# A gated recurrence: where its splits, loads and fills stand, and a fifth pair of each layer turned by DMA

## The reference

```python
for i in range(n_layers):          # 6
    gate = ih[i][token]            # (2048, 256), token clamped to the table
    state = jnp.tanh(state + jnp.matmul(state, hh[i]) * gate)
return state
```

## Time and profile before

| what | us |
|---|---|
| median of 3 runs | 105.71 |
| lowest and highest | 105.27, 107.05 |
| the profiled execution | 106.02 |
| its span, first to last instruction | 104.2 |
| PE busy in the span | 87.1 (84%) |
| DVE busy | 79.2 (76%) |
| ACT busy | 73.5 (70%) |
| POOL busy | 65.7 (63%) |

### The profile page before, as it was taken

The page is one execution under the profiler, slowest core; times in us unless marked ns, Lnnn a source line. Parts: engine busy times, 40 slices in busy tenths (PEclk is TensorE's granted clock), DMA queues, the critical chain, the costliest instruction groups (busy, mean ns, idle before and its releaser), DMA issues.

```text
span 104.2 us, 1794 instructions
## 1 busy us (share of the span) xinstructions
PE 87.1 (84%) x650; PEld 74.4 (71%) x650; DVE 79.2 (76%) x127; ACT 73.5 (70%) x129; POOL 65.7 (63%) x60
## 2 busy tenths in 40 slices
PE   5919909895498998987999989999899998999900
PEld 5817608474386896976898978999789897898800
DVE  2179085283979399996979879798897978989990
ACT  4078020891897818799799996999969999667431
POOL 2687787734043008694897939979398893992440
PEclk9995885589999999999999999999999999999998
DMA  3899999999699915542387523555319654095355
GB/s 39 285 367 401 417 388 376 315 307 347 205 215 268 188 36 101 104 79 48 75 58 145 97 60 58 101 101 101 72 29 86 121 101 94 18 130 221 147 201 201
DMA packets 27128, 17.46 MB, mean 168 GB/s; under 512 B 22421, under 2 KB 22677, under 8 KB 27120
## 3 DMA queue, kind: packets, MB, share of 16 engines
q1 hardware_dynamic: 24816, 13.64, 55.2%
q0 software_dynamic: 2304, 3.71, 9.9%
HBM read 19.14 MB, written 2.10 MB: 204 GB/s over the span
## 4 chain that ended last, share of the span: by engine, by line
PE 51%; DMA 16%; DVE 13%; issue 9%; SPq 3%; ACT 3%; POOL 2%; POOLq 0%; DVEq 0%
PE products L278 38%; PE turned L310 7%; DMA state<-in_state_rows 6%; DVE sums L434 5%; DMA gates<-in_gate_rows,index 5%; PE products L270 5%; DMA w_full<-in_weights 5%; DVE sums L442 4%; ACT gates L336 1%; POOL sums L262 1%; DVE split_rows L455 1%; DVE split_cols L448 1%; ACT state L372 1%; SPq L190 1%; POOL gates L255 1%
## 5 line engine op out<-in xcount | busy, mean ns | idle before, releaser
L262 POOL TENSOR_TENSOR sums<-sums,state 128x512 f32<-128x512 f32 x37 | 46.8, 1274 | 21.4 <-DVE sums L434 20.5
L278 PE MATMUL products<-w_head,split_cols 128*128 128x256 f16 x316 | 54.8, 273 | 1.5 <-issue 1.5
L372 ACT ACTIVATE state<-sums 128x512 f32<-128x512 f32 (+1 forms) x49 | 30.2, 619 | 19.9 <-DVE sums L442 10.9
L278 PE MATMUL products<-w_rest,split_cols 128*128 128x256 f16 x158 | 43.1, 273 | 0.0
L278 PEld LDWEIGHTS products<-w_head,split_cols 128*128 128x128 f16 x316 | 30.9, 98 | 5.8 <-issue 2.3
L434 DVE SCALAR_TENSOR_TENSOR sums<-products,w_down,gates 128x512 f32<-128x512 f32 (+1 forms) x40 | 29.3, 735 | 0.3 <-PE products L278 0.2
L270 PE MATMUL products<-w_full,first_cols 128*128 128x256 f32 x64 | 20.1, 471 | 8.7 <-DMA first_cols<-in_state_cols 6.0
L270 PEld LDWEIGHTS products<-w_full,first_cols 128*128 128x128 f32 x64 | 14.5, 237 | 13.6 <-DMA first_cols<-in_state_cols 7.4
L255 POOL DMA_INDIRECT gates<-in_gate_rows,index x13 | 14.3, 1099 | 10.2 <-ACT gates L336 6.8
L278 PEld LDWEIGHTS products<-w_rest,split_cols 128*128 128x128 f16 x158 | 15.4, 98 | 1.7
L455 DVE SCALAR_TENSOR_TENSOR split_rows<-copies,split_rows 128x512 f16<-128x512 f32 x19 | 13.0, 686 | 3.9 <-ACT split_rows L360 3.7
(11 more groups left out here) (30 smaller groups left out, 28.5 us busy)
## 6 DMA issues: line engine op xcount, KB each, us to landing
first_cols<-in_state_cols SPq DMA_DIRECT2D x8, 256.0 KB, 5.0
state<-in_state_rows SPq DMA_DIRECT2D x8, 256.0 KB, 5.9
out<-state SPq DMA_DIRECT2D x7, 256.0 KB, 2.0
w_full<-in_weights SPq DMA_DIRECT2D x6, 256.0 KB, 5.2
last_row<-in_gate_rows SPq DMA_DIRECT2D x1, 768.0 KB, 4.6
split_cols<-split_rows SPq DMA_TRANSPOSE x19, 3.1
gates<-in_gate_rows,index POOLq DMA_INDIRECT x16, 5.5
out<-state SPq DMA_DIRECT2D x2, 128.0 KB, 1.9
```

The costliest lines, as they stand in the source:

```text
L262: nc.gpsimd.tensor_tensor(sums[:, q], sums[:, q], pair_rows(state, q), ALU.add).then_inc(pool_added, 1)
L278: last = nc.tensor.matmul(bank[:, j, :], split_cols[:, q, s, j, k, :], w[:, l - 1, k * HID:(k + 1) * HID], start=(n == 0), stop=(n == len( ...
L372: nc.scalar.activation(pair_rows(state, q)[:, cut], sums[:, q, cut], ACT.Tanh).then_inc(state_ready, 1)
```

## The change

- Pair 4 of the layers 0 to 4 is turned by DMA too, so there are five turns by DMA in a layer and three by PE. Unlike the other four, pair 4 gets no second tanh into PSUM: its head and its rest are made from `state` in SBUF. `copied`, `state_copies`, `rests_with_copy` and `split_from` count and choose accordingly.
- SP loads the columns one step further ahead (`load_cols(2)` before the steps), one layer of weights with each step's loads instead of two, and the last two pairs of rows together at step 5.
- Six fills on DVE and four on ACT stand before the steps (five and three before), then ACT fills tile 13 after step 0 and tile 15 after step 1, DVE tile 14 after step 0.
- The head of the next layer's weights is made three steps earlier (9, 17, 25, 33), its rest likewise (10, 18, 26, 34). The second sum product stands at step 8.
- Pair 6 of the last layer is added on DVE, not POOL.

```diff
--- before.py
+++ after.py
@@ -33,7 +33,9 @@
     END = STEPS - 1


-    DMA_PAIRS = (1, 3, 5, 7)
+    DMA_PAIRS = (1, 3, 4, 5, 7)
+
+    COPY_PAIRS = (1, 3, 5, 7)
     LAST_TURN = (LAST - 1, PAIRS - 1)

     TURN_LAG = 3
@@ -41,20 +43,20 @@
     REST_LAG, REST_ROWS_LAG = 4, 2


-    LAST_ON_DVE = (3, 5, 7)
+    LAST_ON_DVE = (3, 5, 6, 7)

     WHOLE = 3
-    ACT_FILLS = {-1: (4, 7, 10), 1: (12,), 3: (14,)}
-    DVE_FILLS = {-1: (3, 5, 6, 8, 9), 0: (11,), 2: (13,), 3: (15,)}
+    ACT_FILLS = {-1: (4, 6, 9, 11), 0: (13,), 1: (15,)}
+    DVE_FILLS = {-1: (3, 5, 7, 8, 10, 12), 0: (14,)}


     GROUPS = ((0, 1), (1, SPLIT))
     SUMS_AT = {0: 0, 2: 1, 3: 2, 4: 3, 5: 4}
-    TOTALS_AT = {3: 0, 9: 1}
-    HEADS_AT = {3: 0, 12: 1, 20: 2, 28: 3, 36: 4}
-    RESTS_AT = {4: 0, 13: 1, 21: 2, 29: 3, 37: 4}
+    TOTALS_AT = {3: 0, 8: 1}
+    HEADS_AT = {3: 0, 9: 1, 17: 2, 25: 3, 33: 4}
+    RESTS_AT = {4: 0, 10: 1, 18: 2, 26: 3, 34: 4}

     WARM = 9
     TOP = 14
@@ -70,6 +72,16 @@

     def by_pe(i):
         return order[i][0] < LAST and not by_dma(i)
+
+    def copied(i):
+        return by_dma(i) and order[i][1] in COPY_PAIRS
+
+    def state_copies(i):
+        return sum(copied(n) for n in range(i + 1))
+
+
+    def rests_with_copy(n):
+        return dma_turns([i for i in range(STEPS) if copied(i)][n - 1])

     def on_pool(i):
         layer, q = order[i]
@@ -179,7 +191,10 @@
             return turned[(pe_turns(i) - 1) % TURNED]

         def copy_bank(i):
-            return copies[(dma_turns(i) - 1) % COPIES]
+            return copies[(state_copies(i) - 1) % COPIES]
+
+        def split_from(i):
+            return copy_bank(i)[:, :, :] if copied(i) else pair_rows(state, order[i][1])

         block = ctx.enter_context(nc.Block())

@@ -202,18 +217,16 @@
             load_weights(0)
             load_cols(1)
             load_rows(0)
+            load_cols(2)
             for i in range(STEPS):
-                if i + 2 < PAIRS:
+                if i + 3 < PAIRS:
                     sp.wait_ge(product_ready, i + 1)
-                    load_cols(i + 2)
+                    load_cols(i + 3)
                     load_rows(i + 1)
-                    if i == 0:
-                        load_weights(1)
-                    elif i <= 2:
-                        load_weights(2 * i)
-                        load_weights(2 * i + 1)
-                elif i + 2 == PAIRS:
+                    load_weights(i + 1)
+                elif i + 3 == PAIRS:
                     load_rows(i + 1)
+                    load_rows(i + 2)
                 if i >= LOAD_LAG and by_dma(i - LOAD_LAG):
                     q = order[i - LOAD_LAG][1]
                     sp.wait_ge(rest_rows_ready, dma_turns(i - LOAD_LAG))
@@ -356,8 +369,11 @@

             def make_head_rows(i):
                 q = order[i][1]
-                act.wait_ge(copy_ready, dma_turns(i))
-                nc.scalar.activation(split_rows[:, q, 0], copy_bank(i)[:, :, :], ACT.Copy,
+                if copied(i):
+                    act.wait_ge(copy_ready, state_copies(i))
+                else:
+                    act.wait_ge(state_ready, i + 1)
+                nc.scalar.activation(split_rows[:, q, 0], split_from(i), ACT.Copy,
                                      scale=STATE_SCALE).then_inc(head_rows_ready, 1)

             def new_state(i):
@@ -370,9 +386,9 @@
                     if n >= 1:
                         act.wait_ge(vector_added, vector_adds(i) + n)
                     nc.scalar.activation(pair_rows(state, q)[:, cut], sums[:, q, cut], ACT.Tanh).then_inc(state_ready, 1)
-                if by_dma(i):
-                    if dma_turns(i) > COPIES:
-                        act.wait_ge(rest_rows_ready, dma_turns(i) - COPIES)
+                if copied(i):
+                    if state_copies(i) > COPIES:
+                        act.wait_ge(rest_rows_ready, rests_with_copy(state_copies(i) - COPIES))
                     nc.scalar.activation(copy_bank(i)[:, :, :], sums[:, q], ACT.Tanh).then_inc(copy_ready, 1)

             for t in ACT_FILLS[-1]:
@@ -452,7 +468,7 @@
             def make_rest_rows(i):
                 q = order[i][1]
                 dve.wait_ge(head_rows_ready, dma_turns(i))
-                nc.vector.scalar_tensor_tensor(out=split_rows[:, q, 1], in0=copy_bank(i)[:, :, :], scalar=STATE_SCALE,
+                nc.vector.scalar_tensor_tensor(out=split_rows[:, q, 1], in0=split_from(i), scalar=STATE_SCALE,
                                                in1=split_rows[:, q, 0], op0=ALU.mult,
                                                op1=ALU.subtract).then_inc(rest_rows_ready, 1)

```

## The result

| | before | after |
|---|---|---|
| median of 4 runs, us | 105.53 | 112.38 |
| lowest and highest | 105.27, 107.05 | 111.02, 112.98 |
| profiled execution and its span | 106.02, 104.2 | 112.30, 110.5 |

The ratio is 1.061, with a 95% interval of 1.049 to 1.074. Single executions of one kernel can take some per cent longer than the rest at a lower granted clock; all ratios here leave these out, while the medians are over all executions. The forecast was 98.6 us, and 112.38 lies 10 us above the end of the range.

A forecast was written before the change was run, and what follows sets the result against it. Loads were taken to bound the kernel to about 37 us, PE from 44.91 to 93.84, DVE the end. Savings 4.2 + 2.8 + 0.1 = 7.1 us off the profiled 106.02 gave 98.9, as a median 98.6; range 96.0 to 102.3.

The forecast's parts named there:

- the chain is PE's own: From 44.91 to 93.84 us PE's own work was taken to set the layer, busy 12.45 of 12.74 us.
- The four turns, -1.8: In PE's chain, dropping pair 4's turn by PE from four layers saves 4 x 0.44 = 1.8 us.
- DVE and the lock: Two DVE instructions per layer may wait for POOL's add; half an add, twice, is absorbed by 1.57 us of DVE idle.
- rival (4): Slower: both new DVE instructions wait a whole POOL add, 2.54 us a layer, giving 110.9 us; chance 0.03.
- a swap at 0.06 us: In each layer, DVE's rest of pair 4 from SBUF instead of PSUM costs 0.06 us more.
- The stalls, -2.1: Weights three steps earlier remove PE's stalls before layers (1.5 us) and restarts (0.6); half of 2.1 us was counted.
- The front, -4.2: Until step 7: earlier gathers and loads, all landed between 31.3 and 34.1 us, bring step 7's gated 4.2 us earlier.
- are issued earlier too: In the front, the last rows, issued by 31.28 before, no longer wait for a product of their own.
- The point at which the prediction called itself wrong: The prediction is wrong if the last gather still lands after 34 us, or a layer stays over 12.4.
- PE is no obstacle: In the front, with columns one step ahead, PE's product of step 7 ends well before its gates need it.
- I take this piece as rigid: From step 7's gates to PE's turn at 44.91 us: earlier gates make that turn earlier too.
- The end, -0.1: Last adds: one whole DVE add more (0.69 us) against a lost wait for POOL (0.78 us), -0.1 us.

The follow-up runs named there:

- e9: Kernel before, with only one of pair 4's four PE transposes in layers 1 to 4; executions between 104.95 and 107.74 us, no ratio.
- e10: Kernel before, with the later layers' weights' head at steps 10, 18, 26, 34 and rest at 12, 20, 28, 36; 106.17 us, ratio 1.004.
- e12: Kernel before plus pair 4 turned by DMA from state, its rest first in a step, weights' head and rest at steps 10 and 12 and so on; 106.64 us, 1.004.
- e6: Kernel before plus pair 4 turned by DMA from state, its rest put ahead of the PE-turned pair's rest in a step; 108.35 us, ratio 1.014.
- e7: Kernel before plus one unused DVE copy from PSUM ahead of pair 7's gated in layers 1 to 4; 108.38 us, ratio 1.014.
- e5: Kernel before plus pair 4 turned by DMA from state, at late places: head three steps behind, rest four, transpose five; 113.29 us, no interval.
- e3: Changed kernel with four pairs turned by DMA, without the fifth, keeping the new fills, loads and weights' steps; 107.50 us, ratio 1.013.
- e13: Changed kernel with four pairs by DMA, last row loads ahead of the first transpose, which waits until last rows and gates have landed; 107.71 us, 1.017.
- e11: Changed kernel with four pairs by DMA and the last row loads ahead of SP's first DMA transpose, which is not held; 108.76 us, 1.023.
- e14: Changed kernel with four pairs by DMA, rows first, first transpose held until inputs land, and the old weights' steps; 108.24 us, no interval.

## Why the prediction was wrong

**The step that failed** is the first section's "From there to 93.84 us the chain is PE's own" with "A layer takes 12.74 us, in which PE is busy for 12.45". PE was nearly full and had a stall of only 0.28, and I read that as a bound with a small hitch. It was the other way: what ended the hitch was the bound. What closes each layer is a loop of 12.74 us that PE meets once: the rest of the weights and the `gated` on DVE, the adds on POOL, tanh and head on ACT, the rest on DVE, and so on to the next layer's weights. The kernel before was balanced to 2%, and the busy share could not tell which of two nearly equal bounds was the longer. e9 tells it: 0.33 us less PE work, 0.33 more stall.

**The four turns, -1.8.** Measured: nothing. In e9 PE's work fell and the layer did not; e10 and e12 take 12.85 and 12.88 with four and with five pairs. The instructions went as said.

**DVE and the lock.** That half a POOL add, twice, "is just absorbed" by 1.57 us of idle time of DVE is the second failure, and the more costly. That idle time was waiting for ACT inside the loop, at other places than the new instruction; 0.60 us of work between the `gated` of pairs 6 and 7 was paid whole (e6, e7). Measured is 0.60 for the rest of pair 4 as work and 0.70 for its wait for POOL, 1.30 a layer. The wait itself lay inside my bounds of 0 and 1.27. So rival (4), slower, with a chance of 0.03, was the one that came: 110.9 against 112.38. Its condition, that DVE must lose more than its idle time and a whole add for each of two instructions, was wrong; one instruction and half an add were enough. That its number came near is luck: it had 9.5 of loss and 4.3 of gain, where by the first table the layers lost 7.4 and the front and the end gave 1.1. I also took the second rest for a swap at 0.06 us. It has the old one's length, but stands two steps earlier in the program, and place counted ten times as much as length.

The Trainium skill, page SBUF — State Buffer, section Who interferes with whom, says that a DVE instruction with two SBUF inputs and a GpSimd instruction that reads SBUF contend, and the later is blocked. The traces agree, also for this kind of instruction: 1.38 and 1.72 where DVE came second, 0.68 where it came first and POOL took 1.65 (e5: 0.69, and 1.77 on POOL). I had weighed the rule and given it half; what was wrong was to set it against idle time.

**The stalls, -2.1, half taken.** PE's stall before a layer did go, but a layer became 0.27 longer (e3), not shorter. At the earlier steps the loop holds three ACT instructions more (a head, a tanh and a second tanh, 1.50 us in all, as from 70.97 to 72.46 in the changed kernel) and one POOL add of 1.27 less, and DVE waits 0.71 for the head of the weights (0.44 before). With e10's steps it is 12.85, still no gain. Which arrangement would open the loop stays open.

**The front, -4.2.** Measured: -0.2 in one trace of each kernel, and step 7 varies by 3 us between executions; but over the six kernels with the new loads and no held transpose it is never before 36.4. The first half of the reasoning held: the last gather started at 24.78, forecast 24.8, and where nothing disturbed them, the loads were in at 33.85 (e13), inside my 31.3 to 34.1. Two terms were missing. One is SP's queue: the last loads of rows stood behind a transpose whose issue took 5.07 us, so that "are issued earlier too" came down to 29.02 against 30.37. The other is the time to landing: I used 5.40 for a gather, and beside transposes it was 10.4 in the changed kernel and 12.2 in e11. By e3 and e11 these two stand behind one another, each hiding the other. The point at which the prediction called itself wrong, a last gather landing after 34, was met in the changed kernel itself (24.78 and 10.4 more, 35.2), though there the wait for the rows of pair 6, until 35.8, was the longer one. "PE is no obstacle" failed as well once these two were out of the way: in e13 the `gated` of step 7 waits 0.31 for its product.

"I take this piece as rigid: if step 7's gates come earlier, PE's turn at 44.91 does too" held where nothing but the front's own variation moved step 7: in e6 and e7 it stands at 35.84 and 38.85, and step 15 comes 14.18 later in both; in the kernel before and in e9 it is 36.73 and 38.35, with 13.59 and 13.60. It broke only where the transposes were held: in e13 and e14 step 7 came 1.9 and 2.0 us earlier, and step 15 came 0.5 and 1.2 later, for the reasons above.

Of the 2.2 us that layer 1 is longer in the changed kernel, 1.56 is what every layer lost. The other 0.6 agrees in size with a wait on the chain: the first early rest of the weights, at 44.53, waits 1.32 for ACT's head, where the later ones wait 0.71 (1.32 and 0.71 in e3 too). No run tests it by itself.

**The end, -0.1,** was right, as a mechanism and in size: from `gated` of step 43 to the last tanh 7.68 us before and 7.54 after, with one long add (the whole one of step 45) and not two:

```profile
103.61 1.20 DVE L458 TENSOR_TENSOR sums<-sums,state 128x512 f32<-128x512 f32 x1
...
107.49 0.42 DVE L458 TENSOR_TENSOR sums<-sums,state 128x256 f32<-128x256 f32 x1
```

The median for an add is 0.69; the last half add took 0.42, as forecast.

**Open.** Why the issue and the landing of a transpose take that long while loads are in flight is not shown; only that they do, and that its absence frees the gather. The loop's path rests on releasers inferred from semaphore events and on e6, e7 and e9; not every link was changed by itself.

## What to carry to other kernels

A busy share of 98% does not prove that an engine is the bound: take a little work off it, or add a known piece to another engine, and see whether the period follows, before you pay for relief. Where a chain of waits runs along one nearly full engine, follow what ended its small stall as well. In a pipeline of in-order engines, idle time is slack only at the place where it stands; work put ahead of pair 7's instruction on the loop was paid whole, ahead of pair 1's by half. A two-operand SBUF instruction on VectorE beside GpSimd is cheap or dear by a tenth of a microsecond of start order, so such a placement holds only as long as nothing before it moves.
